# Ternarising the last six of sixteen weight strips on VectorE instead of on ScalarE and GpSimd

## The reference

```python
xn = layernorm(x)                                   # over the last axis, eps 1e-5
# recurrent branch
a = tanh(xn @ Wa.T + ba); b = tanh(xn @ Wb.T + bb)  # [T, 64]
h[t] = a[t] * h[t-1] + b[t]                         # scan over t
attn = xn + h @ Wout.T + bout
# ternary branch
scale = mean(abs(weight))                           # weight is [2048, 2048]
w_t = clip(round(weight / (scale + 1e-10)), -1, 1)
ffn = xn @ (w_t * scale).T + bias
y = x + attn + ffn
```

## Time and profile before

| | us |
|---|---|
| time, median of 3 runs | 820.49 (819.96 to 820.77) |
| the profiled execution, its own time | 819.61 |
| span of its slowest core (core 2) | 818.0 |
| spans of the 8 cores | 815.9 to 818.0 |
| busy on core 2: PE / DVE / ACT / POOL | 576.7 / 368.8 / 228.9 / 268.4 |

### The profile page before, as it was taken

One profiled execution on the slowest core, in us unless ns is written; L12 is line 12 of the kernel. 1 busy time (PEld: TensorE's weight loads), 2 busy tenths in 40 slices (PEclk: granted clock), 3 DMA queues, 4 the chain that ended last, 5 costly groups with the idle time before them and its releaser, 6 DMA issues.

```text
span 818.0 us, 10776 instructions; the slowest of 8 cores (815.9 to 818.0 us)
## 1 busy us (share of the span) xinstructions
PE 576.7 (70%) x3484; PEld 303.3 (37%) x3548; DVE 368.8 (45%) x321; ACT 228.9 (28%) x246; POOL 268.4 (33%) x754
## 2 busy tenths in 40 slices
PE   0100341110005999999999999999999999999996
PEld 0100331010003445444454444454444544444542
DVE  0278782000503264544545545545446455455431
ACT  2200344234313223233223232232232232322320
POOL 1000124644584233332234332334332334323320
PEclk9999999999999999999999999999999999999998
DMA  7998384120001222234332344222443233432212
GB/s 214 304 343 295 105 261 148 51 83 20 0 0 53 104 103 104 104 119 181 113 104 103 111 152 151 103 103 104 133 158 123 103 105 109 161 142 104 104 52 103
DMA packets 17069, 102.99 MB, mean 126 GB/s; under 512 B 4566, under 2 KB 4598, under 8 KB 4598
## 3 DMA queue, kind: packets, MB, share of 16 engines
q1 hardware_dynamic: 9590, 51.96, 19.9%
q0 software_dynamic: 7424, 50.34, 16.1%
HBM read 68.73 MB, written 33.55 MB: 125 GB/s over the span
## 4 chain that ended last, share of the span: by engine, by line
PE 59%; ACT 9%; POOL 8%; DMA 7%; DVE 4%; ACTq 4%; issue 4%; DVEq 2%; SPq 2%; POOLq 1%
PE pffn L525 14%; PE pffn L537 14%; PE pffn L533 13%; PE pffn L522 13%; DMA wtile<-wf 4%; ACT xnT L298 4%; ACTq L297 3%; PE pab L510 3%; DVE wpart L316 2%; PE ptr L547 2%; SPq L169 2%; ACT xnT L239 1%; ACT xnT L236 1%; DMA vv<-wf 1%; ACT xnT L294 1%
## 5 line engine op out<-in xcount | busy, mean ns | idle before, releaser
L525 PE MATMUL pffn<-w_rhs,xnT 128*128 128x512 bf16 x512 | 194.1, 379 | 1.9 <-issue 0.2
L537 PE MATMUL pffn<-w_rhs,xnT 128*128 128x512 bf16 x512 | 194.0, 379 | 1.7
L533 PE MATMUL pffn<-w_rhs,xnT 128*128 128x512 bf16 x480 | 181.9, 379 | 0.0
L522 PE MATMUL pffn<-w_rhs,xnT 128*128 128x512 bf16 x480 | 181.9, 379 | 0.0
L372 DVE TENSOR_REDUCE sums<-sx 128x1 f32<-128x2048 f32 x32 | 73.1, 2286 | 226.5 <-DMA sx<-x 147.0
L480 PE MATMUL ptr<-sidn,wbn 128*128 128x128 bf16 x256 | 29.8, 309 | 120.9 <-DVE wbn L358 23.8
L294 ACT COPY xnT<-ptr 128x1024 bf16<-128x1024 bf16 x31 | 31.4, 1012 | 243.1 <-PE ptr L547 243.1
L276 ACT ACTIVATE xnb<-sx,nmr,yr 128x2048 bf16<-128x2048 f32 x31 | 64.9, 2094 | 101.6 <-POOLq L835 101.5
L408 DVE SCALAR_TENSOR_TENSOR outb<-pffn,negs,vv 128x1024 f32<-128x1024 f32 x32 | 41.1, 1284 | 114.3 <-PE pffn L563 110.4
L801 POOL TENSOR_SCALAR mm_<-sums 128x1 f32<-128x1 f32 x32 | 8.3, 260 | 235.2 <-DVE sqscr L374 233.0
L374 DVE SCALAR_TENSOR_TENSOR sqscr<-sx 128x2048 f32<-128x2048 f32 x32 | 75.8, 2369 | 0.0
(11 more groups left out here) (129 smaller groups left out, 598.4 us busy)
## 6 DMA issues: line engine op xcount, KB each, us to landing
sx<-x SPq DMA_DIRECT2D x32, 1024.0 KB, 5.4
y<-outb POOLq DMA_DIRECT2D x32, 1024.0 KB, 5.7
outb<-wf POOLq DMA_DIRECT2D x11, 1024.0 KB, 6.4
wtile<-wf SPq DMA_DIRECT2D x8, 1024.0 KB, 10.1
vv<-wf SPq DMA_DIRECT2D x8, 1024.0 KB, 10.1
sqscr<-wf POOLq DMA_DIRECT2D x5, 1024.0 KB, 6.9
wasb<-wa SPq DMA_DIRECT2D x1, 512.0 KB
wosb<-wout SPq DMA_DIRECT2D x16, 32.0 KB, 9.7
```

What stands on the lines that cost most here:

```text
L522: tensor.matmul(pffn[:, 0:512], lhs, w_rhs[:, 2048 * c:2048 * c + 512], start=st_, stop=False)
L525: tensor.matmul(pffn[:, 512:1024], lhs, w_rhs[:, 2048 * c + 512:2048 * c + 1024], start=st_, stop=False)
L533: tensor.matmul(pffn[:, 1024:1536], lhs, w_rhs[:, 2048 * c + 1024:2048 * c + 1536], start=st_, stop=False)
L537: ins = tensor.matmul(pffn[:, 1536:2048], lhs, w_rhs[:, 2048 * c + 1536:2048 * c + 2048], start=st_, stop=False)
```

## The change

The loop at L347 on DVE runs over all 16 strips instead of 10. ACT's two sign instructions per strip and POOL's two tensor instructions per strip are removed for strips 10 to 15, with the semaphores `s_sgn2` and `s_acp`; PE waits for `s_tern` for all strips; the refill of a ring slot waits for `s_tern` for all strips, and POOL's unrolled stream becomes a loop of 16 DMA issues with the same destinations in the same order. The waits of `sums_sqs(0)` and of the first two evictions on `s_sgn2` are gone, since DVE's own order now covers them.

```diff
@@ scalar @@
             for j in range(NW):
-                if j >= 10:
...
-                    scalar.wait_ge(s_wlb[sl], 16 * (j // 3 + 1))
-                    scalar.wait_ge(s_thr, 1)
-                    if j - 10 >= 1:
-                        scalar.wait_ge(s_acp, j - 10)
-                    scalar.drain()
-                    scalar.sign(xnT[:, 0:D], buf[:, so:so + D],
-                                bias=nthr128[:, :])
-                    scalar.drain()
-                    scalar.sign(xnT[:, D:2 * D], buf[:, so:so + D],
-                                bias=thr128[:, :]).then_inc(s_sgn2, 1)
                 for grp in range(2):
@@ vector @@
-            for j in range(10):
+            for j in range(NW):
...
-                if j == 0:
-                    vector.wait_ge(s_sgn2, 5)
...
-                if k <= 1:
-                    vector.wait_ge(s_sgn2, 6)
@@ tensor @@
-                    if j < 10:
-                        tensor.wait_ge(s_tern, j + 1)
-                    else:
-                        tensor.wait_ge(s_acp, j - 10 + 1)
+                    tensor.wait_ge(s_tern, j + 1)
@@ gpsimd, one of the six unrolled strips @@
-            g.wait_ge(s_sgn2, 11 - 9)
...
-            g.drain()
-            g.tensor_tensor(g_sb[:, :], xnT[:, 0:D], xnT[:, D:2 * D], OP.add)
-            g.wait_ge(s_wtr, 2 * 11 - 2)
-            g.drain()
-            g.tensor_scalar(wbn[:, (11 % 2) * D:(11 % 2 + 1) * D],
-                            g_sb[:, :], -0.5, None, OP.mult).then_inc(s_acp, 1)
...
+            for j in range(NW):
+                if j >= 3:
+                    g.wait_ge(s_tern, j - 2)
+                sl = j % 3
+                buf = outb if sl < 2 else sqscr
+                so = (sl % 2) * D if sl < 2 else 0
+                g.dma_start(out=buf[:, so:so + D],
+                            in_=wf_d[128 * j:128 * (j + 1), :]
+                            ).then_inc(s_wlb[sl], 16)
```

More of the change, by code:

```diff
@@ L573, in _ @@
             g.memset(two_i[:, :], 2)
[L574 to L617, removed]
-            sl, = [4 % 3]
-            buf = outb if sl < 2 else sqscr
-            so = (sl % 2) * D if sl < 2 else 0
-            g.dma_start(out=buf[:, so:so + D],
-                        in_=wf_d[128 * 4:128 * (4 + 1), :]
-                        ).then_inc(s_wlb[sl], 16)
-            if 5 >= 3 and 5 - 3 < 10:
-                g.wait_ge(s_tern, 5 - 2)
-            elif 5 >= 3:
-                g.wait_ge(s_sgn2, 5 - 12)
@@ L628, in _ @@
-            sl, = [5 % 3]
-            buf = outb if sl < 2 else sqscr
-            so = (sl % 2) * D if sl < 2 else 0
-            g.dma_start(out=buf[:, so:so + D],
-                        in_=wf_d[128 * 5:128 * (5 + 1), :]
-                        ).then_inc(s_wlb[sl], 16)
-            if 6 >= 3 and 6 - 3 < 10:
-                g.wait_ge(s_tern, 6 - 2)
-            elif 6 >= 3:
-                g.wait_ge(s_sgn2, 6 - 12)
-            sl, = [6 % 3]
-            buf = outb if sl < 2 else sqscr
@@ L719, in _ @@
-            so = (sl % 2) * D if sl < 2 else 0
-            g.dma_start(out=buf[:, so:so + D],
-                        in_=wf_d[128 * 13:128 * (13 + 1), :]
-                        ).then_inc(s_wlb[sl], 16)
-            g.wait_ge(s_sgn2, 11 - 9)
-            if 11 == 10:
-                g.wait_ge(s_tern, 10)
-            g.drain()
-            g.tensor_tensor(g_sb[:, :], xnT[:, 0:D], xnT[:, D:2 * D], OP.add)
-            g.wait_ge(s_wtr, 2 * 11 - 2)
-            g.drain()
-            g.tensor_scalar(wbn[:, (11 % 2) * D:(11 % 2 + 1) * D],
-                            g_sb[:, :], -0.5, None, OP.mult).then_inc(s_acp, 1)
@@ L745, in _ @@
-            g.drain()
-            g.tensor_tensor(g_sb[:, :], xnT[:, 0:D], xnT[:, D:2 * D], OP.add)
-            g.wait_ge(s_wtr, 2 * 12 - 2)
-            g.drain()
-            g.tensor_scalar(wbn[:, (12 % 2) * D:(12 % 2 + 1) * D],
-                            g_sb[:, :], -0.5, None, OP.mult).then_inc(s_acp, 1)
-            if 15 >= 3 and 15 - 3 < 10:
-                g.wait_ge(s_tern, 15 - 2)
-            elif 15 >= 3:
-                g.wait_ge(s_sgn2, 15 - 12)
-            sl, = [15 % 3]
-            buf = outb if sl < 2 else sqscr
@@ L757, in _ @@
-            so = (sl % 2) * D if sl < 2 else 0
-            g.dma_start(out=buf[:, so:so + D],
-                        in_=wf_d[128 * 15:128 * (15 + 1), :]
-                        ).then_inc(s_wlb[sl], 16)
-            g.wait_ge(s_sgn2, 13 - 9)
-            if 13 == 10:
-                g.wait_ge(s_tern, 10)
-            g.drain()
-            g.tensor_tensor(g_sb[:, :], xnT[:, 0:D], xnT[:, D:2 * D], OP.add)
-            g.wait_ge(s_wtr, 2 * 13 - 2)
-            g.drain()
-            g.tensor_scalar(wbn[:, (13 % 2) * D:(13 % 2 + 1) * D],
-                            g_sb[:, :], -0.5, None, OP.mult).then_inc(s_acp, 1)
@@ L782, in _ @@
-            g.drain()
-            g.tensor_tensor(g_sb[:, :], xnT[:, 0:D], xnT[:, D:2 * D], OP.add)
-            g.wait_ge(s_wtr, 2 * 15 - 2)
-            g.drain()
-            g.tensor_scalar(wbn[:, (15 % 2) * D:(15 % 2 + 1) * D],
-                            g_sb[:, :], -0.5, None, OP.mult).then_inc(s_acp, 1)
+            for j in range(NW):
[7 more added lines that the diff above has]
+                            ).then_inc(s_wlb[sl], 16)
```

103 lines of the change are left out of this document (removed).

## The result

| | before | after |
|---|---|---|
| median, us | 820.5 | 736.7 |
| profiled execution, own time | 819.61 | 736.52 |
| span of its slowest core (core 2 in both) | 818.0 | 734.9 |

The ratio of the times is 0.8979, with a 95% interval of 0.8968 to 0.8990: 83.8 us are gone. The forecast was 733.5, so the gain came, and it was 3.2 us smaller than the forecast said.

A forecast was written before the change was run, and what follows sets the result against it. The main loop sets its own length and starts at the first normalisation, held back by six strips in a closed ACT-POOL loop. That start moves 87.0 us earlier: 819.61 - 87.0 = 732.6, plus 0.9 gives 733.5; range 729.5 to 739.5.

The forecast's parts named there:

- strip 15 to the first chain: DVE's row sums of tile 0 enter the path: a 0.08 step plus 4.85 us before POOL's first chain.
- The strips: DVE does strips 10 to 15 at its own pace, 6 x 3.81 = 22.86 us, ending at 149.82.
- The stalls: DVE waiting for late loads in the last six strips: bounded 0 to 5.0 us, taken at 1.0.
- POOL's queue: 16 small DMAs and their drain end at 152.1, 2.6 us before the row sums, so nothing is charged.
- Rival C: POOL's small DMAs become the bound, shut out by two-input DVE instructions: 741.2 us; chance 6%.
- The exclusion: L374 of tile 1 on DVE holds up a tiny POOL instruction of the first chain: 2.1 us.
- Rival D: L374 does not hold up the chain's tiny POOL instructions and no load is late: 730.4 us; chance 20%.
- The main loop: After the first normalisation everything keeps its distances, same instructions; nothing given for PE's shorter pause.
- Rival E: Slower than before, through a slow matmul rate on PE far into the main loop: say 825 us; chance 0.5%.
- Rival F: The six strips were not on the path, so the change gains nothing: 820.5 us; chance 0.5%.
- The POOL wait: POOL idle for some 2 us before its first L575, released by DVE's L358.
- two signs of being wrong: Time from L238 to the end differs from before, or the wait before L238 ends on something other than the chain.

The follow-up runs named there:

- the run with 13: Kernel before with 13 instead of 10 strips on DVE, the last three still on ACT and POOL: 779.6 us, ratio 0.9509.
- five buffers: Changed kernel with five instead of three ring buffers for the ternary strips, the two halves of wtile added: 735.7 us, ratio 0.8966.
- the run in which DVE is idle there: Changed kernel with DVE's row sums of tile 1 moved behind the first chain and vv of tile 0: 734.5 us, ratio 0.8957.
- the first statistics early: Changed kernel with row sums, first chain and normalisation of x tile 0 moved early, and its vv ahead of tile 1's row sums: 723.0 us, ratio 0.8801.

## Why the prediction was right, and by how much it was off

Set out for core 2, whose profiled execution carries the sum:

| step of the sum | predicted, us | measured, us | difference |
|---|---|---|---|
| end of strip 9 | 126.96 | 127.06 | +0.1 |
| strips 10 to 15, with stalls | 22.86 + 1.0 | 24.33 | +0.5 |
| strip 15 to the first chain | 4.93 | 7.48 | +2.55 |
| first chain to the normalisation | 7.27 + 2.1 | 9.21 | -0.2 |
| normalisation to the end of the span | 565.9 | 566.8 | +0.9 |
| own time of the execution | 732.6 | 736.52 | +3.9 |
| median above that execution | 0.9 | 0.2 | -0.7 |

**The strips.** Right in mechanism and in price: 3.81 us for each on DVE, and 13.6 us gained for each in the run with 13. The stalls were bounded from 0 to 5.0 and taken at 1.0; on core 2, beyond the usual step of 0.1, they were 0.33 and 0.78 in the six, and the unexplained pause makes it 1.5. Core 6 had the most over the whole stage. That every core then ran at 59.8 us with five buffers shows that a stall was a single late load, and not the memory's rate. The 1.0 was taken from one stall of 1.66 us; two smaller ones came, so that the size is near is in part luck.

**POOL's queue.** This is the term that failed. The prediction let the small DMAs end at 150.2 (they ended at 150.0) and then "with the 1.9 us drain at 152.1", and charged nothing. (Its 2.6 us for L353 are those of two strips, where its text says three; two L339 fell into the issues.) But in POOL's code the wait for the row sums stands ahead of that drain. The drain could not begin under cover. It began at 156.0, in the path, and it was 2.6 us longer than a drain without DMAs before it. The 1.89 us were there to be seen in the earlier trace rows, as "issue" in front of L801; I gave them the right name and put them on the wrong side of the wait. The size was short too: the 1.89 stood behind 16 DMAs, and here there were 32. A drain behind the small DMAs, which does run under cover, brought the start to 4.85. Rival C, which had the small DMAs held up by L358, is refuted: 16 of them took 9.35 us instead of 7.73, with two L339 and most of three L344 beside them, and issuing them early changed nothing. The line's own view on core 2 (durations in ns, min/median/max) has them go on at their usual pace except where an L339 stood in the way:

```profile
L564 POOL DMA_DIRECT2D wocv<-cneg x16: 487/495/1444, 140.7 to 149.5; - x16
```

**The exclusion.** Right in mechanism. Taken at 2.1 of a possible 2.28, it measured 1.56 in the first instruction of the chain; with the 0.35 of the gap behind it, which the prediction didn't have, the chain is 1.9 longer than 7.27. That the total comes within 0.2 us is partly luck, since the late start had left L358 running ahead for 0.6 us. The mechanism is shown by the run in which DVE is idle there: 0.23 instead of 1.78. Rival D is out. The rule of the Trainium skill's page "SBUF — State Buffer", section "SBUF: two separate sides", that was weighed in the prediction fits nearly all of it: a two-input DVE instruction held a small POOL instruction in every kernel in which the two met (1.78, 1.87 and 2.03 us in three of them), and L344, two-input too, did not stop the DMA issues. One row of the kernel before, of DVE on core 2 and the same on cores 0, 4 and 7, does not fit a pair held for the whole instruction:

```profile
214.90 3.33 DVE L374 SCALAR_TENSOR_TENSOR sqscr<-sx 128x2048 f32<-128x2048 f32 x1
```

POOL's L777 was running when it started and ran until 217.81, so behind it L374 would have ended at about 220.1 (217.81 + 2.28). It ended at 218.23.

**The main loop.** It was to have the same 565.9 us and took 566.8. The chain of waits shows most of the difference at its beginning, against the earlier trace rows:

```profile
174.93 0.63 PE pffn L504
175.57 0.43 PE pffn L501
176.00 0.42 PE pffn L504
176.42 0.22 PE pffn L501
```

Before, only the first matmul took longer than 0.22 us; now the first three do. At 0.43 us for 512 columns TensorE is at 1.2 GHz and at 0.22 at 2.4; the mean granted clock of the core is the same in both, 0.996. Counted matmul by matmul, from the fifth on each starts 0.6 us later behind the first than before, so this is 0.6 of the 0.9 us; the other 0.3 falls later in the loop, and its place is open. The PE pause ahead was 16.8 us against 17.0. The change need not be the cause: over the eight cores the stretch from the normalisation to the end took 565.4 to 566.9 us before (mean 566.2) and 565.9 to 566.8 after (mean 566.5), and core 2 was simply one of the three cores with an early rise before. What sets the moment of the rise isn't settled. Rival E is out, since this ends after three matmuls. Rival F is refuted by the result itself.

The prediction had also said how it would show: one or two idle pieces of 1 to 2 us on DVE from late loads, a POOL wait of some 2 us that DVE's row sums release, one instruction of about 2 us in the chain, the normalisation at about 165 us. The first came smaller (0.43 and 0.88 us), the instruction came as said (1.78), the normalisation 3 us later (168.08). The POOL wait did not: POOL's idle time before L575 was 8.85 us and was released by "issue", and that was the signature of the missed term. Of its two signs of being wrong, one showed weakly: the time from the normalisation to the end differed, by 0.9 us on core 2, which is within the spread of the cores of the kernel before.

## What to carry to other kernels

When two engines hand one buffer back and forth, price the whole loop between two uses of that buffer; its full turn (17.5 us here) is what the helper's help costs, and an engine that does the job alone in 3.8 us is far better off. When a queue is said to be covered, check on which side of the wait its drains stand: a drain behind DMA issues belongs directly behind them if the queue is idle there, and not where another issue would have to wait for the landing (the small DMAs came 6 to 7 us later that way). And when a stage is shortened, what had been hidden under it moves into the path; here 16.7 us of statistics could be moved to where the engines still waited for the first loads, and that was worth another 15 us (736.7 against 721.8).

## What the runs showed of the hardware

A drain on GpSimd behind its own issue of a 1 MB load stands until the load has landed: one that landed 5.6 us after its issue kept the queue 5.95 us from the issue's end, and over seven cores the queue went on 1.28 to 1.36 us behind the landing. When everything has landed before the drain begins, it takes about 0.082 us for each DMA issued since the drain before: 0.26 us more for 3, 1.07 for 13, 1.39 for 16, 2.37 for 29, 2.63 for 32. Behind 16 small DMAs just issued the two parts are not simply added (1.9 us in all, see above). No source line shows this time; the profile calls it "issue" or puts it to POOL's queue.

A two-input DVE instruction on 2048 elements (2.28 us) keeps a small POOL instruction standing until it is over, once for a whole chain of them: 1.78 us beside one, 0.23 without. A one-input row sum beside the same chain did not.

The first small tensor_tensor of POOL in the chain came 0.50 us after the instruction ahead of it in the changed kernel, 0.32 to 0.38 in the three runs with one extra drain (0.16 on one core), and 0.15 in later chains. With two small instructions ahead the gap did not go away, it moved ahead of the chain (0.51 to 0.55 us). It is not simply a cost of first use, nor of a drain behind many DMAs: with the first statistics early it was 0.15 in the first chain, where it was the first use too, and 0.15 in the second, behind 29 DMAs. Its cause is open.
